# Adding the turned window sums one group later in a four-part graph network kernel

## The reference, cut to what matters

```
# second network
m_in = concatenate([h_node[src], h_node[dst], h_edge], axis=-1)
m = silu(m_in @ W1 + b1) @ W2 + b2
agg = segment_sum(m, dst, num_segments=3125)
# third network, for l in range(3)
x = concatenate([h[src], e], axis=1) @ W1[l].T + b1[l]      # 256 channels
x = (x - mean(x)) * rsqrt(var(x) + 1e-5) * gamma[l] + beta[l]
m = relu(x) @ W2[l].T + b2[l]
h = segment_sum(m, dst, num_segments=3125)
```

## Time and profile before

| | |
|---|---|
| median of three runs | 4864.7 us |
| the profiled execution's own time | 4827.65 us |
| its span, first to last instruction | 4826.2 us |
| TensorE matmul busy | 2815.5 us (58%) |
| VectorE busy | 2115.7 us (44%) |
| ScalarE busy | 1578.0 us (33%) |
| GpSimd busy | 2134.1 us (44%) |
| mean granted TensorE clock | 0.726 of full speed |

### The profile page before, as it was taken

How to read it: one execution, slowest core, us unless ns; L and a number is a source line. 1 busy time by engine, 2 the same in 40 slices (tenths; PEclk the granted TensorE clock), 3 DMA queues, 4 the chain that set the end, 5 groups by cost and what they waited for, 6 DMA issues and landing times.

```text
span 4826.2 us, 57244 instructions
## 1 busy us (share of the span) xinstructions
PE 2815.5 (58%) x12415; PEld 1700.8 (35%) x12415; DVE 2115.7 (44%) x2957; ACT 1578.0 (33%) x3332; POOL 2134.1 (44%) x2027
## 2 busy tenths in 40 slices
PE   4667946776777444333687433335873433358797
PEld 1123434444444232222454222223542322235443
DVE  8876832233233533333673333335743333347601
ACT  6776222222222222222462222223632222236410
POOL 1005624544541355555463555554645555536200
PEclk7568965555555767667898677767996776769998
DMA  1002033333331355555484565554855565538500
GB/s 55 0 0 86 1 100 115 104 108 103 100 110 36 128 191 195 188 183 187 154 268 137 192 200 191 184 189 135 268 168 182 195 203 189 186 120 268 197 1 14
DMA packets 271498, 679.44 MB, mean 141 GB/s; under 512 B 48481, under 2 KB 81174, under 8 KB 270006
## 3 DMA queue, kind: packets, MB, share of 16 engines
q1 hardware_dynamic: 155574, 332.76, 21.7%
q0 software_dynamic: 73216, 190.95, 13.8%
q10 hardware_dynamic: 42624, 154.70, 8.5%
HBM read 502.27 MB, written 175.94 MB: 141 GB/s over the span
## 4 chain that ended last, share of the span: by engine, by line
PE 30%; another core or an unknown queue 25%; issue 20%; DVE 15%; ACT 4%; DVEq 4%; ACTq 1%; DMA 0%; POOL 0%; SPq 0%; POOLq 0%
PE psum L629 7%; PE psum L458 6%; PE psum L769 6%; DVE acc L1218 4%; PE psum L731 3%; PE psum L505 3%; PE psum L472 3%; DVEq L909 2%; DVE tN L1270 1%; DVE tN L1226 1%; DVE acc L922 1%; PE psum L565 1%; DVEq L402 1%; PE psum L733 1%
## 5 line engine op out<-in xcount | busy, mean ns | idle before, releaser
L769 PE MATMUL psum<-w_all,region 128*128 128x256 f32 x2496 | 830.8, 495 | 1307.3 <-ACT region L1472 751.8
L769 PEld LDWEIGHTS psum<-w_all,region 128*128 128x128 f32 x2496 | 598.0, 250 | 1539.9 <-issue 927.8
L382 POOL DMA_INDIRECT region<-tab,idx_ring x624 | 589.8, 945 | 783.7 <-issue 752.6
L382 POOL DMA_INDIRECT tN<-tab,idx_ring x624 | 589.9, 945 | 361.2 <-issue 188.0
L1226 DVE TENSOR_TENSOR region<-region,psum 128x1024 f32<-128x1024 f32 x156 | 190.2, 1219 | 938.1 <-remote 648.9
L1639 POOL TENSOR_TENSOR region<-node_no,dst_rel 128x256 f32<-128x256 f32 x312 | 384.2, 1232 | 324.3 <-ACT region L1516 241.0
L1486 ACT ACTIVATE psum<-region 128x1024 f32<-128x1024 f32 x156 | 160.2, 1027 | 911.0 <-DVE acc L1218 438.5
L1218 DVE TENSOR_TENSOR acc<-acc,psum 128x1024 f32<-128x1024 f32 x312 | 379.5, 1216 | 53.0 <-issue 30.7
L731 PE MATMUL psum<-w_all,region 128*128 128x128 f32 x832 | 326.3, 493 | 112.4 <-issue 74.0
L1226 DVE TENSOR_TENSOR tN<-tN,psum 128x1024 f32<-128x1024 f32 x156 | 190.2, 1219 | 436.1 <-remote 250.8
L382 POOL DMA_INDIRECT region<-tabs,idx_ring x208 | 201.8, 970 | 301.6 <-issue 301.6
(11 more groups left out here) (267 smaller groups left out, 4110.0 us busy)
## 6 DMA issues: line engine op xcount, KB each, us to landing
region<-e_t SPq DMA_DIRECT2D x416, 256.0 KB
pre_dram<-region ACTq DMA_DIRECT2D x144, 512.0 KB
pre_dram<-tN ACTq DMA_DIRECT2D x144, 512.0 KB
region<-pre_dram SPq DMA_DIRECT2D x144, 512.0 KB, 4.6
tN<-pre_dram SPq DMA_DIRECT2D x144, 512.0 KB, 4.5
tA<-dst_row SPq DMA_DIRECT2D x78, 256.0 KB
adj_kept<-region SPq DMA_DIRECT2D x5, 2000.0 KB, 15.1
region<-adj_kept SPq DMA_DIRECT2D x5, 2000.0 KB, 15.7
```

The source lines that it names most:

```text
L382: pool.indirect_dma_start(m_ring[j][:, c, at:at + width], None, table[:, :], bass.IndirectOffsetOnAxis(ap=idx_at(j, k)[:, c:c + 1], axis=0 ...
L769: mm = pe.matmul(banks[:, 2 * (j % 2) + c // 2, (c % 2) * 256:(c % 2) * 256 + 256], e_ring[:, j % E_SLOTS, c * D:(c + 1) * D], W(f"ee{l}") ...
```

## The change

LAG becomes 3. Window add(g) now takes what turn(g-2) wrote and adds it at the window start of group g-3; which of the two PSUM places it reads changes accordingly. Since turn(g) writes the place that window add(g) reads, turn(g) now waits for window adds 0 to g, one more than before. Both places of turned sums are cleared before a pass, since one more add has no sums yet, and after the loop there are three more adds and no longer two. The table of window starts has one more leading zero. The number of places (two of acc_ps, two of win_ring, two of window_ps) stays.

```diff
-LAG = 2
+LAG = 3
@@ pe_turn_window
             pe.wait_ge(S["win_out"], T["win_out"] + b + 1)
-            pe.wait_ge(S["sc_add"], T["sc_add"] + b)
+            pe.wait_ge(S["sc_add"], T["sc_add"] + b + LAG - 2)
@@ dve_window
-            dve.wait_ge(S["win_t"], T["win_t"] + a)
+            dve.wait_ge(S["win_t"], T["win_t"] + a - (LAG - 2))
             dve.wait_ge(S["sc_add"], T["sc_add"] + a)
@@ before block 1, and the same in each layer ahead of a summing pass
-            v.did(dve.memset(window_ps(0), 0.0))
+            for n in range(LAG - 1):
+                v.did(dve.memset(window_ps(n), 0.0))
@@ add1 in block 1
-                dve_window(dve, T, g, w0, j % 2, 1)
+                dve_window(dve, T, g, w0, (j + LAG) % 2, 1)
@@ loop of a summing pass
-                        dve_window(dve, T, g, w0, j % 2, 2)
+                        dve_window(dve, T, g, w0, (j + LAG) % 2, 2)
@@ after the loop of a summing pass (and with 1 for 2 after that of block 1)
                 for a in range(NG, NG + LAG):
-                    dve_window(dve, T, a, dve_window_start(dve, a - LAG), a % 2, 2)
+                    dve_window(dve, T, a, dve_window_start(dve, a - LAG), (a + LAG) % 2, 2)
```

More of the change, by code:

```diff
@@ L1182, in dve_program @@
             for a in range(NG, NG + LAG):
-                dve_window(dve, T, a, dve_window_start(dve, a - LAG), a % 2, 1)
+                dve_window(dve, T, a, dve_window_start(dve, a - LAG), (a + LAG) % 2, 1)
             count_block1(T)
```

## The result

The changed kernel takes 4754.05 us (median of six runs) against 4860.31 us for the kernel before in the same jobs (six runs): a ratio of 0.9775, with a 95% interval of 0.9751 to 0.9799. That is 106 us less; 95 were forecast, and 4770 us. (A job is a set of runs made together on one chip.) In a later job, unchanged, the ratio was 0.9771 (0.9735 to 0.9807).

A forecast was written before the change was run, and what follows sets the result against it. A two-group loop of waits through VectorE's add was taken to bound the summing passes: 300 x (1.95 - 1.63) = 96 us gained, +1 for small parts, so 4864.7 - 95 = 4770 us, range 4735 to 4828.

The forecast's parts named there:

- What bound: Summing passes: no engine full; a loop of waits through VectorE's add takes 3.98 us for two groups, 1.95 a group on average.
- TensorE's floor of 1.60: Summing passes: TensorE's queue, full from turn to turn, cannot go below 1.60 us a group; 1.63 was taken.
- VectorE with GpSimd, 1.56 at worst: Summing passes: VectorE needs 1.42 us a group, 1.56 at worst when GpSimd's subtraction falls on a message.
- Transfers, 1.56: Summing passes: loads of 512 KB a group fill the DMA engines at near 1.56 us a group, as late as TensorE.
- Rival 1: Summing passes: loads take the wait's place, idle time shows before L1270, 1.79 us a group, 4817 us in all; chance 0.18.
- The start of a pass: Until the clock rises, turn to turn takes 2.95 us with TensorE in line: nothing gained, bounds 0 to 4 us.
- The wait that comes: TensorE's turn(g) now waits for add(g); segment(g) covers it by about 1.2 us, so cost taken as 0.
- Block 1, taken as 0: Most remote waits before block 1's adds would be met again at sum L1165: gain 0, ends -40 and +40 us.
- Small parts, +1: One more clear in each of four passes and one more add after the loop: about +1 us, ends 0 and 4.
- The base: Whole kernel: the profiled execution's 4827.65 us gives 4733; the difference to the median, 4864.7, is carried over, giving 4770.
- The range: Whole time 4735 to 4828 us, taking in the loads rival's 4817, the spread of medians and the best ends (105 + 20).
- The signs named: Two-half adds idle under 60 us, turn to turn 1.60 to 1.65, passes 30 to 33 us shorter, DMA share 0.95 or so.

The follow-up runs named there:

- e4 repeat: Kernel before with an extra 0.27 us clear (128x256 values) on VectorE ahead of each summing-pass message: 16.43 to 16.53 us for eight groups; 4005.24 us against 3971.36.
- e9: Kernel before with the turn of one half left out: 14.57 to 14.73 us for eight groups.
- e7: Changed kernel with the turn of one half left out, two of twelve TensorE products a group: 12.42 us for eight groups.
- e8: Changed kernel with the turn of one half and half of each load left out: 12.42 us for eight groups.
- e5: Changed kernel with an extra 0.27 us clear on VectorE ahead of each summing-pass message: 12.82 us for eight groups, unchanged.
- e6: Changed kernel loading only half of each group's values (256 KB for 512 KB): 12.82 us for eight groups; 3865.29 us against 3971.36 for the kernel before.
- e4: Kernel before with an extra small clear (128x32 values) on VectorE ahead of each summing-pass message: 15.63 to 15.73 us for eight groups.

## Why the prediction was right, point by point

- **What bound.** Right. The loop through VectorE's add held the passes: a longer clear on VectorE (e4 repeat) and a shorter turn (e9) both moved the old step, and opening the loop in either of two ways gave the same 12.82 us.
- **TensorE's floor of 1.60.** Right to the hundredth: 12.82 / 8 = 1.602. Here is the term that was mis-sized. I took 1.63, for places where four close floors meet; they cost nothing. (1.63 - 1.602) x 300 = 8 us of the 11 by which the forecast gain fell short; the 3 that remain are within the spread of the runs. (The forecast time was 16 us too long; the rest of that is the median of the kernel before, 4864.7 us in the first three runs and 4860.31 in six.)
- **VectorE with GpSimd, 1.56 at worst.** Right: 1.55 in e7 and e8.
- **Transfers, 1.56, and the rule of the Trainium skill.** The term was too large. The changed kernel runs at a share of 0.92 and 1.60 us, so by the same sum full occupation is 1.47 us. The landing went from 4.6 to 4.8 and 5.1 us, so three loads or so are under way at a time:

```profile
tN<-pre_dram SPq DMA_DIRECT2D x32, 512.0 KB, 5.1
region<-pre_dram SPq DMA_DIRECT2D x30, 512.0 KB, 4.8
```

  Loads of 512 KB reached 337 GB/s in e7 at 1.55 us a group. The estimate from the Trainium skill's "DMA: Bandwidth & Descriptors" (Bandwidth), under 326 GB/s for a transfer below 1 MiB, so over 1.61 us, did not hold here, where loads overlap. Rival 1 is out.
- **The start of a pass.** Turn to turn was 2.95 us at the low clock (0.50) as before, nothing gained there. The length of a start varies: the first eight groups took 13.9 to 18.0 us in the two profiles of the changed kernel, 18.1 to 20.3 in those of the old one. Beyond 300 x (1.95 - 1.602) = 104 us the first pair of profiles gained 5.5 us in the passes, over the 4 named, the second 0.5.
- **The wait that comes.** Cost nothing, as argued: TensorE is busy 1.00 of the time.
- **Block 1, taken as 0.** Right, and so is the reason, that a wait taken away is met again; the place was not the one named. I had it met at the sum L1165. In the first profiles the idle time before that sum grew from 358.2 to 396.4 us only, and the larger part stands before the first split of the table (L1152, now L1153):

```profile
L1152 DVE TENSOR_TENSOR region<-region 128x128 f32<-128x128 f32 x104 | 29.6, 284 | 1.9 <-ACT region L1428 1.6 <-issue 0.3
```

```profile
L1153 DVE TENSOR_TENSOR region<-region 128x128 f32<-128x128 f32 x104 | 29.7, 286 | 124.0 <-issue 97.8 <-ACT region L1430 26.2
```

  What ends these waits is mostly not seen ("issue"), so the cause stays open. On the other chip the place was the sum: in one job e4's repeat (old lag) and e5 (new lag) both had block 1 587.1 us long, with TensorE busy all of it. VectorE's waits there, from 680 to 1255 us, first with the old lag and then with the new:

```profile
DVE tN L1165 <- PE psum L733: 104.0, 51, 2.2
DVE region L1165 <- PE psum L733: 90.8, 50, 2.2
...
DVE acc L480 <- PE psum L472: 29.6, 100, 0.5
```

```profile
DVE tN L1166 <- PE psum L733: 124.8, 51, 2.8
DVE region L1166 <- PE psum L733: 110.1, 50, 2.8
```

  The 29.6 us before the adds are gone, and the waits for edge products have grown by 20.8 + 19.3 = 40.1 us.
- **Small parts, +1.** Nearer +3. After a summing pass the adds now stand so:

```profile
2541.62 0.29 DVE L480 TENSOR_TENSOR acc<-acc,psum 128x128 f32 x1 [0.74 <-PE psum L472]
2543.00 0.29 DVE L480 TENSOR_TENSOR acc<-acc,psum 128x128 f32 x1 [1.10 <-PE psum L472]
2543.82 0.29 DVE L480 TENSOR_TENSOR acc<-acc,psum 128x128 f32 x1 [0.53 <-PE psum L472]
2544.18 0.06 DVE L1287 MEMSET small<- 128x1 f32 x1
```

  From the last message (2538.49) to that last line is 5.69 us; it was 4.89 before (2559.62 to 2564.51). The extra add costs 0.8 us a pass, in all three, not 0.3.
- **The base.** Carrying the difference to the median was right. From the profiled execution alone the sum gave 4733 us, and the changed kernel's profile spans 4752.5: the first profile had short gathered stages.
- **The range.** Its best ends come to 4864.7 - 105 - 20 = 4740 us, not 4735; the result lies inside either.
- **The signs named.** Idle time before the two-half adds fell to 39.7 us (under 60 was named), TensorE is busy throughout, the DMA engines at 0.92 with 324 GB/s, and block 1 is within 20 us of its old length. One sign missed: the passes were to be shorter by 30 to 33 us and were by 35 to 38, since it was worked out from the 1.63.

## What to carry to other kernels

When no engine is full, walk the timeline from one instruction to its like a few groups later and write down the loop of waits. Its length over the number of groups it spans is the step. To widen the span by one group took here two changed wait counts, one more cleared place and one more add after the loop, 0.8 us a pass. Then list what each queue needs when nothing waits: the largest of these is the new step. Here it was met without a surcharge, with the others 3% and more below. A wait ahead of an instruction is worth removing only where what follows is not waited for anyway: 143 us of idle time left the adds of block 1, and block 1 became no shorter.

## What the runs showed of the hardware that was not expected

- In one of the jobs the kernel before took 3971.36 us where it took about 4860 in the others. It was not profiled there, but edited kernels were. Where e5 and e6 keep the changed kernel's step it was the same to 0.1 us in eight groups, but block 1 took 587.1 us for 856, and each edge pass 515 for some 720; TensorE was busy throughout block 1 there, at a clock of 0.50 (line below, of e5), and the remote waits of the earlier trace rows were gone. What changes the gathered stages so much is open; nothing here tried it. The edits compared in that job, e6 against the kernel before, differ by 106.1 us (one run each), so the gain is one of microseconds and not of per cent.

```profile
680.00:1255.00 575.00, 575.00 (x2637) 371.14 (x2638) 239.44 (x608) 191.08 (x553) 386.73 (x404) 0.50 0.53 150
```

- VectorE's message (128x1024 values, two SBUF inputs) and GpSimd's subtraction (128x256) took turns in e7 and e8, where both queues are full: each pair takes 1.55 us, 1.08 from the subtraction's end to the message's and 0.47 from there to the subtraction's. With a clear of 0.27 us ahead of each message (e5) the message stayed at 1.16 us.
- A clear of 0.27 us cost the queue 0.13 us (e5) and the loop 0.21 us (e4's repeat), one of 0.09 us next to nothing (1.43 for 1.42 us, e4): the records of neighbouring instructions overlap.
